# Counts brought back in part earlier, slots summed on PE, norm and recurrent weights moved ahead, in a graph network of four layers

## The reference

```python
x = _layernorm(x + _L0_gnn_ref(x, edge_index, ...))   # two GIN convolutions: h = x + segment_sum(x[src], dst), two dense layers
x = _layernorm(x + _L1_gnn_ref(x, edge_index, ...))   # two attention convolutions over the edges, log_softmax at the end
x = _layernorm(x + _L2_gnn_ref(x, src, dst, ...))     # four recurrent blocks
x = _layernorm(x + _L3_gnn_ref(x, edge_attr_64, src, dst, ...))  # messages h[dst] * W(rbf), summed at src
```

```python
x = h * norm_src[:, None]
agg = jax.ops.segment_sum(x[src], dst, num_segments=n)
g = agg * norm_dst[:, None] @ gcn_w[b] + gcn_b[b]
gi = g @ gru_w_ih[b].T + gru_b_ih[b]
```

## Time and profile before

| | us |
|---|---|
| median of three runs | 6434.16 (6433.62 to 6436.32) |
| profiled execution, its own time | 6430.39 |
| span of the profiled execution | 6428.8 |
| PE busy | 4263.4 (66%) |
| DVE busy | 3787.8 (59%) |
| POOL busy | 3580.3 (56%) |
| ACT busy | 1190.0 (19%) |

### The profile page before, as it was taken

One profiled execution on the slowest core, in us unless ns is written; L12 is line 12 of the kernel. 1 busy time (PEld: TensorE's weight loads), 2 busy tenths in 40 slices (PEclk: granted clock), 3 DMA queues, 4 the chain that ended last, 5 costly groups with the idle time before them and its releaser, 6 DMA issues. The chain is left out here.

```text
span 6428.8 us, 102457 instructions
## 1 busy us (share of the span) xinstructions
PE 4263.4 (66%) x26702; PEld 2979.1 (46%) x26703; DVE 3787.8 (59%) x8560; ACT 1190.0 (19%) x1987; POOL 3580.3 (56%) x3658
## 2 busy tenths in 40 slices
PE   0666667395267777776256666663777778777884
PEld 0111114263156565665245566652555456565663
DVE  8777772154589898898556666665111235555553
ACT  0111111012211111111211221121211222222221
POOL 1222224502377777774277777770666667777772
PEclk9999999698589999998567676676888888889886
DMA  4000004200244444444233333335222222222233
GB/s 192 12 15 14 12 15 182 63 21 30 72 127 116 124 117 124 123 116 83 78 81 81 80 81 80 79 67 180 60 63 61 66 69 78 78 78 78 78 78 42
DMA packets 332968, 513.66 MB, mean 80 GB/s; under 512 B 104565, under 2 KB 245919, under 8 KB 322966
## 3 DMA queue, kind: packets, MB, share of 16 engines
q0 software_dynamic: 130656, 290.33, 17.9%
q1 hardware_dynamic: 202166, 221.78, 10.7%
HBM read 409.97 MB, written 101.86 MB: 80 GB/s over the span
## 5 line engine op out<-in xcount | busy, mean ns | idle before, releaser
L1027 POOL DMA_INDIRECT e_ring<-att_rows,e_near x1792 | 1845.3, 1030 | 550.5 <-issue 483.6
L1094 PE MATMUL e_psum<-e_ring,e_whole_pick 128*128 128x264 f32 (+1 forms) x3584 | 864.5, 395 | 303.8 <-DVE e_ring L1254 293.8
L1784 POOL DMA_INDIRECT e_nodes<-x,e_edges x832 | 807.4, 970 | 266.0 <-issue 242.6
L1094 PEld LDWEIGHTS e_psum<-e_ring,e_whole_pick 128*128 128x128 f32 x3584 | 664.2, 230 | 430.7 <-issue 204.2
L1049 PE MATMUL e_px<-t_parts,e_pick 128*128 x5376 | 694.9, 271 | 111.1 <-DVE e_pick L1156 51.8
L1172 DVE TENSOR_TENSOR e_prod<-e_px,e_ring 128x512 f32<-128x512 f32 x672 | 458.1, 682 | 492.5 <-DMA e_ring<-att_rows,e_near 411.6
L285 PE MATMUL b_acc<-b_pick_key,b_pick_lo 128*128 128x416 bf16 (+1 forms) x1960 | 496.7, 340 | 169.5 <-DVE b_pick_key L256 151.1
L1049 PEld LDWEIGHTS e_px<-t_parts,e_pick 128*128 128x128 bf16 x5376 | 455.8, 108 | 204.2 <-issue 134.5
L1701 POOL DMA_INDIRECT sorted<-rx_held,rx_index x432 | 426.4, 987 | 221.8 <-issue 212.1
L355 PE MATMUL r_pa<-gru_counts,gru_parts 128*128 x3000 | 452.0, 317 | 135.5 <-DMA r_bh<-in_gru_bh 117.7
L1136 ACT ACTIVATE e_whole_pick<-e_pturn 128x512 f32<-128x512 bf16 x448 | 266.4, 595 | 1318.0 <-PE e_pturn L1085 1294.3
(11 more groups left out here) (336 smaller groups left out, 6294.3 us busy)
## 6 DMA issues: line engine op xcount, KB each, us to landing
e_relb<-place SPq DMA_DIRECT2D x56, 1024.0 KB
e_ring<-att_rows,e_near POOLq DMA_INDIRECT x1792
sorted<-o_fill SPq DMA_DIRECT2D x11, 2508.0 KB
e_edges<-sorted SPq DMA_DIRECT2D x209, 132.0 KB
kept<-gin_counts SPq DMA_DIRECT2D x5, 4000.0 KB, 35.3
gru_counts<-kept SPq DMA_DIRECT2D x5, 4000.0 KB
rx_held<-in_edge_rows POOLq DMA_DIRECT2D x52, 297.0 KB
e_nodes<-x,e_edges POOLq DMA_INDIRECT x832
```

Of the source, the lines that this page charges most:

```text
L1027: pool.indirect_dma_start(out=ring[:, s, r, 0:wd + HEADS], out_offset=None, in_=xrows, in_offset=bass.IndirectOffsetOnAxis(ap=near[:, s, r ...
L1094: mm = pe.matmul(psum[q % 2][:, 0:RING], whole_pick[:, q % 2, c, :], ring[:, s, q * G + c, :], start=(c == 0), stop=(c == G - 1))
L1784: pool.indirect_dma_start(out=nodes[:, q, u, :], out_offset=None, in_=source, in_offset=bass.IndirectOffsetOnAxis(ap=edges[:, q, u, RBF + ...
```

## The change

1. `edge_order`: PE sums `rank` over the tiles, by 50 FP32 matmuls of 391 columns against the identity into two banks, each pair behind its rank step; DVE copies the two banks into the integer slots. The reduction and the cast go.
2. The room for the counts is split in two, and so are the tiles (`Pieces` picks the half). The first two pieces are brought back within the first block of the second attention, behind the first two loads of x on SP's queue; the other three as before. Their semaphores now belong to an outer scope.
3. `softmax_norm`: PE reports after each piece. DVE applies the norm first, takes the identity out of the diagonal blocks piece by piece, and clips the sums ahead of the last five. The reciprocal of `to_scale` leaves the stage.
4. `gru_block`: the weights are loaded ahead of loads 3 and 4 of the state. In block 0, DVE takes the reciprocal of 640 columns of `to_scale` at the top of each group.

```diff
@@ -344,6 +344,21 @@
                 dve.wait_ge(self.loaded[step % self.slots], 16 * (step // self.slots + 1))
                 dve.tensor_tensor(s, s, self.scale[:, g * GT:(g + 1) * GT].unsqueeze(2).broadcast_to([P, GT, P]),
                                   ALU.mult).then_inc(self.scaled, 1)
+
+
+class Pieces:
+
+
+    def __init__(self, early, late, split):
+        self.early, self.late, self.split = early, late, split
+
+    def __getitem__(self, key):
+        p, j, d = key
+        if isinstance(j, slice):
+            if j.start < self.split:
+                return self.early[p, j, d]
+            return self.late[p, j.start - self.split:j.stop - self.split, d]
+        return self.early[p, j, d] if j < self.split else self.late[p, j - self.split, d]
 
 
 def sum_neighbours(pe, AT, parts, banks, f, g, half, lo):
@@ -502,6 +517,7 @@
 
 
 HEADS = 4
+EARLY = 2
 SC = 400
 G = 4
 ROWS = 32
@@ -666,7 +682,7 @@
                 mm.then_inc(back, 1)
 
 
-def attention(nc, K, D, source, fin, w, att_l, att_r, bias, ch, target, elu):
+def attention(nc, K, D, source, fin, w, att_l, att_r, bias, ch, target, elu, early=None, back=None):
 
 
     FB = fin // P
@@ -713,6 +729,10 @@
                     sp.dma_start(biasb[:, :], bias.partition_broadcast(P)).then_inc(weights, 16)
                     for g in range(2):
                         sp.dma_start(x[:, g, :, :], rows(source, g * GT, GT)).then_inc(loaded[g], 16)
+                    if early is not None:
+                        for i in range(EARLY):
+                            sp.dma_start(early[:, i * GT:(i + 1) * GT, :], D["kept"][:, i * GT:(i + 1) * GT, :]
+                                         ).then_inc(back[i], 16)
                     for g in range(NG):
                         sp.wait_ge(sums, g + 1)
                         sp.dma_start(rows(xrows, g * GT, GT), line[:, g % 2, :, :]).then_inc(stored, 16)
@@ -1308,7 +1328,7 @@
             steps(dve, step)
 
 
-def softmax_norm(nc, K, D, source, residual, target, AT, kept, outdeg, from_scale, to_scale):
+def softmax_norm(nc, K, D, source, residual, target, AT, kept, back, outdeg, from_scale, to_scale):
 
 
     Q = NP // SC
@@ -1325,14 +1345,13 @@
         psum = [m.ps(f"u_psum{q}", [P, BANK]) for q in range(Q)]
         loaded, step, act_step, stored, ready, made, clipped, rooted = (
             m.sem(f"u_{n}") for n in ("loaded", "step", "act_step", "stored", "ready", "made", "clipped", "rooted"))
-        back = [m.sem(f"u_back{i}") for i in range(NG)]
         wide = [P, NT, P]
         with nc.Block() as block:
             @block.sync
             def _(sp):
                 sp.dma_start(v[:, :, :], source.rearrange("(t p) f -> p t f", p=P)).then_inc(loaded, 16)
                 sp.dma_start(x[:, :, :], residual.rearrange("(t p) f -> p t f", p=P)).then_inc(loaded, 16)
-                for i in range(NG):
+                for i in range(EARLY, NG):
                     sp.dma_start(AT[:, i * GT:(i + 1) * GT, :], kept[:, i * GT:(i + 1) * GT, :]).then_inc(back[i], 16)
                 sp.wait_ge(step, 4)
                 sp.dma_start(target.rearrange("(t p) f -> p t f", p=P), x[:, :, :]).then_inc(stored, 16)
@@ -1359,7 +1378,8 @@
                     for q in range(Q):
                         mm = pe.matmul(psum[q][:, 0:SC], ones[:, :], AT[:, j, q * SC:(q + 1) * SC],
                                        start=(j == 0), stop=(j == NT - 1))
-                mm.then_inc(made, 1)
+                    if j % GT == GT - 1:
+                        mm.then_inc(made, 1)
 
             @block.vector
             def _(dve):
@@ -1379,18 +1399,19 @@
                 dve.tensor_tensor(x[:, :, :], x[:, :, :], total[:, :].unsqueeze(2).broadcast_to(wide), ALU.subtract)
                 dve.drain()
                 norm_stats(dve, x, stats, mv, NT).then_inc(step, 1)
-                dve.wait_ge(made, 1)
-                for q in range(Q):
-                    dve.tensor_scalar(to_scale[:, q * SC:(q + 1) * SC], psum[q][:, 0:SC], -1.0, 1.0, ALU.add, ALU.max)
-                dve.drain().then_inc(clipped, 1)
+                dve.wait_ge(act_step, 3)
+                norm_apply(dve, x, mv, NT).then_inc(step, 1)
                 for t in range(NT):
+                    if t % GT == 0:
+                        dve.wait_ge(made, t // GT + 1)
+                    if t == NT - GT:
+                        for q in range(Q):
+                            dve.tensor_scalar(to_scale[:, q * SC:(q + 1) * SC], psum[q][:, 0:SC], -1.0, 1.0, ALU.add, ALU.max)
+                        dve.drain().then_inc(clipped, 1)
                     block_ = AT[:, t, t * P:(t + 1) * P]
                     dve.tensor_tensor(block_, block_, K["identb"][:, :], ALU.subtract)
-                dve.wait_ge(act_step, 3)
-                norm_apply(dve, x, mv, NT).then_inc(step, 1)
                 dve.wait_ge(rooted, 2)
                 dve.reciprocal(from_scale[:, :], from_scale[:, :])
-                dve.reciprocal(to_scale[:, :], to_scale[:, :])
                 dve.drain()
 
 
@@ -1428,13 +1449,15 @@
             @block.sync
             def _(sp):
                 sp.sem_inc(stored, 16)
-                for i in range(NG):
+                for i in range(3):
                     split.load(sp, i)
                 sp.dma_start(wg[:, :], D["gcn_w"][b * P:(b + 1) * P, :]).then_inc(weights, 16)
                 sp.dma_start(wi[:, :], D["gru_w"][b * P:(b + 1) * P, :]).then_inc(weights, 16)
                 sp.dma_start(bg[:, :], D["gcn_b"][b * P:(b + 1) * P, :]).then_inc(weights, 16)
                 sp.dma_start(bi[:, :], D["gru_bi"][b * P:(b + 1) * P, :]).then_inc(weights, 16)
                 sp.dma_start(bh[:, :], D["gru_bh"][b * P:(b + 1) * P, :]).then_inc(weights, 16)
+                for i in range(3, NG):
+                    split.load(sp, i)
                 with sp.Fori(0, NG) as g:
                     if residual is not None:
                         sp.wait_ge(stored, g * 16 + 16)
@@ -1498,6 +1521,9 @@
                 dve.tensor_scalar(brz[:, 1:2], brz[:, 1:2], -1.0, None, ALU.mult)
                 dve.drain().then_inc(biases, 1)
                 with dve.Fori(0, NG) as g:
+                    if b == 0:
+                        dve.reciprocal(to_scale[:, ds(g * GW, GW)], to_scale[:, ds(g * GW, GW)])
+                        dve.drain()
                     for i in range(2):
                         dve.wait_ge(sums, g * 2 + i + 1)
                         dve.tensor_tensor(summed[:, halves[i]], pa[i][:, 0:HW], to_scale[:, ds(g * GW + i * HW, HW)],
@@ -1574,13 +1600,15 @@
         groups = m.sb("o_groups", [P, NT])
         first = m.sb("o_first", [P, NT])
         offset = m.sb("o_offset", [P, NT])
-        slotf = m.sb("o_slotf", [P, NC])
         slot = m.sb("o_slot", [P, NSC], I32)
         src_tile = m.sb("o_src_tile", [1, NHALF + HALVES], I32)
         tile_base = m.sb("o_tile_base", [P, NHALF])
         ppast, pall = (m.ps(f"o_p{n}", [P, BANK]) for n in ("past", "all"))
-        loaded, ready, filled, counted, summed, blank, listed, stored = (
-            m.sem(f"o_{n}") for n in ("loaded", "ready", "filled", "counted", "summed", "blank", "listed", "stored"))
+        pslot = m.ps("o_pslot", [P, 2, BANK])
+        loaded, ready, filled, counted, summed, owned, slotted, blank, listed, stored = (
+            m.sem(f"o_{n}") for n in ("loaded", "ready", "filled", "counted", "summed", "owned", "slotted", "blank",
+                                      "listed", "stored"))
+        parts = ((0, 0, NC // 2), (1, NC // 2, NC))
         with nc.Block() as block:
             @block.sync
             def _(sp):
@@ -1643,17 +1671,17 @@
                 dve.drain()
                 for t in range(NT):
                     dve.scalar_tensor_tensor(out=rank[:, t, :], in0=rank[:, t, :], scalar=offset[:, t:t + 1],
-                                             in1=own[:, t, :], op0=ALU.add, op1=ALU.mult)
+                                             in1=own[:, t, :], op0=ALU.add, op1=ALU.mult).then_inc(owned, 1)
                 dve.wait_ge(ready, 2)
                 for t in range(1, NT):
                     dve.scalar_tensor_tensor(out=tile[:, :], in0=count[:, :], scalar=first[:, t:t + 1], in1=tile[:, :],
                                              op0=ALU.is_ge, op1=ALU.add)
                     dve.drain()
-                dve.tensor_reduce(slotf[:, :], rank[:, :, :].rearrange("p t c -> p c t"), AX_X, ALU.add)
+                dve.wait_ge(slotted, 1)
+                for h, lo, hi in parts:
+                    dve.tensor_copy(slot[:, lo:hi], pslot[:, h, 0:hi - lo])
                 dve.tensor_scalar(tile_base[:, :], tile[:, :], float(P), None, ALU.mult)
                 dve.tensor_copy(src_tile[0:1, HALVES:NHALF + HALVES], tile[0:1, :])
-                dve.drain()
-                dve.tensor_copy(slot[:, :], slotf[:, :])
                 dve.drain().then_inc(listed, 1)
 
             @block.tensor
@@ -1662,6 +1690,12 @@
```

(16 more changed lines are left out.)

## The result

The changed kernel takes **6350.4 us** (median of 4 runs, 6344.5 to 6353.0) against 6435.2 for the kernel before in the same session (4 runs, 6433.6 to 6439.4): a ratio of 0.9866, 95% interval 0.9849 to 0.9883. The forecast was 6349.6, with 6338 to 6366 as its range. That the median is met within 1 us is partly luck: by the profiles the touched stages gained 90.4 us, 5.8 more than forecast, and the untouched ones lost 12.9 that the forecast didn't have.

What follows compares the result with a forecast made beforehand. DVE was taken to bound edge order, the pieces' return and DVE softmax and norm, POOL the recurrent blocks just behind the weights' wait. -32.9 + 0 - 46.4 - 6.3 + 1.0 = -84.6 us, from 6434.2 to 6349.6, range 6338 to 6366.

Steps and rivals of the forecast that it cites:

- Rival B: Recurrent blocks: POOL is no wall, so the blocks give 31 us and the total is 6325 us; chance 0.06.
- Rival C: Edge order: PE is never raised to 2.4 GHz and ends at 137 instead of 106, total 6381 us; chance 0.05.
- rival D: Softmax and norm: the early copies don't bring the sums forward, 19.1 us stay, total 6369 us; chance 0.04.
- rival E: Second attention: the early copies hold up SP's queue, +107 us, total 6457 us; chance 0.02.
- Step 1: Edge order: reduction and cast go, copies of 0.98 us come, PE's 50 matmuls stay hidden; 32.9 us gained.
- Step 2: Second attention: two early copies of 4.1 MB on SP's queue cost 0 us, bounds 0 and +3.
- Step 3: Softmax and norm: three pieces return, norm goes first, reciprocal moves out; DVE ends at 4457.1 instead of 4503.6, 46.4 us gained.
- Step 4: Four recurrent blocks: earlier weights start PE 8.2 us sooner each, but POOL's slack limits the gain to 6.3 us.
- step 5: Behind recurrent block 3: semaphores in the outer scope add a round of barrier and clearing, +1.0 us (0 to 1.3).
- POOL's chain: Recurrent blocks: POOL's sends, a wall just behind the weights' wait; charged 0.5 us a block for weights sharing DMA engines, 2.0.
- The handover: Recurrent block borders: from POOL's last send to the next stage's first load, 4.07 us, read at the first convolution.
- 1 us or less (the fourth by some 4): Recurrent blocks, as a sign: each gets shorter by only this much, though the first half sum comes 8 us sooner.

## Why the prediction was right, point by point

**What bounds each stage** held in all three: DVE in the edge order, the pieces' return and then DVE in softmax and norm, POOL in the recurrent blocks. Rival B (POOL no wall, 6325) is ruled out by the pair with and without 12 sends: the same blocks fall from 182 to 176 us only when POOL is relieved. That holds for chips like the first; on the other chip no such fall was seen. Rival C (PE at 1.2 GHz throughout, 6381) is ruled out by the trace, rival D (the early copies bring nothing, 6369) by the kernel without them, whose stage is 19.4 us longer, and rival E (SP's queue held up, 6457) by the equal 22.6 to 22.9 us from the load of x to the store of rows.

**Step 1, edge order: right, -32.9 of -32.9; the price of PE's work was too high, and since PE is hidden behind DVE it isn't in the sum.** A matmul at speed costs 0.66 us, not the 0.71 scaled by columns from 320-column matmuls, so 50 take 32.9 instead of 35.6. The slow start is there nearly as charged, 35.6 - 32.9 = 2.7 us for the 3 taken: the weight loads stand 0.65 us apart from 66.91 to 70.82 and 0.33 apart from 71.23 on, with loads of 0.34 and 0.19 us. PE ended at 101.7 and not at 104.7. The integer copies cost 1.04 for both, 0.98 taken. Here row and rule were weighed against each other, and the spacing decides for the rule: the granted clock reads 1.00 in every slice of this stretch, yet PE, idle for 57 us but for two small sums, begins at half its later pace, 1.2 against 2.4 GHz. So the Trainium skill, "TensorE: Matmul & The Clock Gate", section on the HAM clock gate, agrees with this trace, and the column doesn't show it.

**Step 2, second attention: right, 0.** The stage's first load to the load of x became 1.1 us longer (an issue of 1.56 instead of 0.42 us), but it did in the kernel without the copies as well (1.19).

**Step 3, softmax and norm: right, -47.0 for -46.4.** The kernels that put one part back give 19.4 for the early copies and 20.3 for the reciprocal; the rest, some 7 us, is the norm and the subtractions moved ahead of the last piece, which was not run by itself.

**Step 4, recurrent blocks: the mechanism right, the size too small: -10.5 together with step 5 instead of -5.3.** Seen from SP's first loads, a block is POOL's chain to its last send and the handover to the next block.

- POOL's chain: taken as 2.0 us longer in four (the weights beside its first loads), measured 178.2, 178.9, 176.9 and 177.2, 711.2 in sum against 713.0: 1.8 shorter, off by 3.8. The charge itself was right: the first send comes 2.2 us later in the four blocks together (34.0 instead of 31.8). What the sum lacked is that the chain from the first send to the last is then 4.1 us shorter (677.2 instead of 681.3). The two kernels without the early copies or with the long reciprocal back have this too (677.6 and 678.1), and the two kernels with late weights, the changed one with the weights back and the one with the new edge order alone, don't (682.9 and 684.3). A part of it is that fewer sends begin beside DVE's steps with two SBUF operands (see below); no run isolates the rest.
- The handover: taken as 4.07 from the first convolution, where it is 4.07 again. Between recurrent blocks it is 3.58, 3.60 and 3.94, so 1.1 less in three. The last is 4.77, with the extra round of step 5 in it, where 5.07 was taken. One price from another stage, used four times, was off by 1.4 in all.
- PE's path: DVE's last step ends 7.9, 7.7, 6.0 and 7.6 us sooner after the block's start, 29 in four, where 33 were taken.
- The blocks are 2.6, 0.7, 1.6 and 5.6 us shorter. The prediction had named "1 us or less (the fourth by some 4)" as its sign, so the first, the third and the fourth gained more than it allowed.
- The reciprocals: 0, as taken. The first half sum waits for its 4.15 us until 4453.52, so in this block it is taken only 6.1 us sooner after the first load, not 8; but PE goes on with the second, which DVE then awaits for 8.02 us; and the sends beside them stay at 0.96:

```profile
4447.75 0.83 DVE L337 TENSOR_TENSOR r_work<-r_work,gru_parts 128x640 f32<-128x640 f32 x1 [0.80 <-ACT gru_parts L324]
...
4448.09 1.32 POOL L1735 DMA_INDIRECT sorted<-rx_held,rx_index  x1 [0.30 <-issue]
4449.71 0.96 POOL L1735 DMA_INDIRECT sorted<-rx_held,rx_index  x1 [0.30 <-issue]
4450.98 0.96 POOL L1735 DMA_INDIRECT sorted<-rx_held,rx_index  x1 [0.30 <-issue]
```

The send at 4448.09 begins while DVE's step at 4447.75, with two SBUF operands, is running (until 4448.58), the two others beside the reciprocal (4449.19 to 4453.34). For an instruction with one SBUF operand the trace agrees with the Trainium skill, "SBUF — State Buffer", on the shared port pair. For two, what the prediction took from it (only the read side is taken, which descriptor writing doesn't need) doesn't fit: a send of 1.32 here, 1.53 in the earlier trace rows, against 0.96. The traces show what decides. In the kernel before, 30 of the 432 sends of the four blocks begin while such a two-operand step of 0.82 us is under way and has over 0.1 us to go; each takes the rest of that step and 0.83 to 0.90 us more, 1.30 on average. The sends beside steps of the same operation with one operand in PSUM (L1503) take 0.96 on average, at most 0.99. The changed kernel has 26 such sends of 1.26 on average, and 16 and 13 of 0.96 and 0.97 beside the PSUM steps and the reciprocals. So a send that begins beside a step with two SBUF operands waits for its end; some 10 us of POOL's chain in four blocks went there before, some 8 after. A send reads its indices from SBUF (`rx_index`); that this is why it waits isn't shown.

**Not forecast: +7.5 us in the edge messages.** There POOL makes 832 gathers one after the other. The row of the groups, of the kernel before and of the changed one:

```profile
L1784 POOL DMA_INDIRECT e_nodes<-x,e_edges x832 | 807.4, 970 | 266.0 <-issue 242.6 <-DMA e_edges<-sorted 23.4
```

```profile
L1818 POOL DMA_INDIRECT e_nodes<-x,e_edges x832 | 813.9, 978 | 265.5 <-issue 238.7 <-DMA e_edges<-sorted 26.8
```

8 ns a gather, 6.5 us in sum. The new edge order seemed the cause, as the kernel with that alone has 979 ns. But the kernel before with 96 sends, which keeps the old edge order, has it too, in both its runs (here the first; it ran on the other chip, where the changed kernel with 96 sends has 978, as it has on the first, and where no trace of the kernel before was taken):

```profile
L1784 POOL DMA_INDIRECT e_nodes<-x,e_edges x832 | 814.3, 979 | 644.8 <-DMA e_edges<-sorted 372.2 <-issue 272.5
```

So the new order seems not to be needed for it. Of the thirteen other traces eleven have 978 or 979, two have 973 and 975 on the other chip (one of them 979 when run again on the first kind), and the kernel before 970, of which there is one trace only. It is more than a chance of that trace: the kernel with the new edge order alone has a median only 25 us below that of before, where its stage is 33 shorter. That it goes by where POOL's loop lies in the program is a guess that fits, since the median gather is 944 or 947 ns in all and the longer ones come in pairs in each pass of the loop (1.13 and 1.16 us on average in the kernel before, 1.22 and 1.16 in the changed one). No run shows it, and the cause stays open. The +4.1 us in the edge passes I don't explain either: the same stage takes 1205.9 to 1213.1 us in the kernels here, and 1209.3 in the changed kernel with 96 sends.

## What to carry to other kernels

Where a wait is removed, look at every engine that must reach the same barrier, with its slack at it: the same edit was worth 10 us with a sender just behind it and 28 without. The wall that is left over is then the next change: POOL's sends moved to where POOL waits (22.7 us in each tile of the counts stage) brought 103 us more, by five constants, on a chip like the first; on the other chip this kernel wasn't run, and the counts stage with only two more sends a tile was some 50 us longer there. And a long operation of one engine at a stage's end is best cut up and put beside another engine's work, as the reciprocal was, at a cost of 1 us at most.

## What the runs showed of the hardware

- PE begins at half its later pace after 57 us of near idleness, while the granted clock reads 1.00 throughout: 0.65 us, then 0.33 between weight loads.
- An indirect send of POOL takes 0.96 us. One that begins while DVE runs a step with two SBUF operands takes the rest of that step and 0.83 to 0.90 us more (up to 1.57 in the kernel before). Beside a step with one operand in PSUM, or beside a reciprocal of 4.15 us, it stays at 0.96.
- The border between two stages with POOL last takes 3.6 to 3.9 us here and 4.07 behind the first convolution.
- One chip ran the same program at 7366 us and another at 6433, with most of the difference in the stages with many row gathers. Stages without them differ as well: in the recurrent blocks it hid an effect of 7 us a block, and the counts stage with 9 sends a tile takes 903 to 908 us there against 856. A comparison of blocks was of use only on chips of one kind.
- The mean of the same gather on POOL is 970 ns in the kernel before and 973 to 979 in the others, at the same median.
